# Dividing by a running sum: an exact reciprocal replaced by a guess and a cubic correction

## The reference, cut to what matters

```
x = x + 0.5 * ffn(layernorm(x));  x = x + attention(layernorm(x));  x = x + 0.5 * ffn(layernorm(x))

# ffn
h = square(relu(einsum('bsd,fd->bsf', x, W_fc)));  y = einsum('bsf,df->bsd', h, W_proj)
# 5 steps of a threshold recurrence on y, spikes counted; result = count / 5

# attention (h = layer_norm(x, gamma, beta))
keys, values = h @ Wk.T + bk, h @ Wv.T + bv
key_att = keys @ Wka.T + bka
keys_weight = exp(key_att / sqrt(128))
keys_weight = keys_weight / cumsum(keys_weight, axis=1)
pooled_keys = cumsum(keys_weight * keys, axis=1)
return pooled_keys * values
```

## Time and profile before

| what | value |
|---|---|
| median of 3 runs | 166.24 us (166.01 to 166.38) |
| the profiled execution | 166.34 us, its span 164.6 us (1.7 us lie around it) |
| granted TensorE clock, mean | 0.985 of full speed |
| busy: PE, DVE, ACT, POOL | 155.0 (94%), 136.8 (83%), 124.9 (76%), 109.5 (67%) us |

### The profile page before, as it was taken

One profiled execution on the slowest core, in us unless ns is written; L12 is line 12 of the kernel. 1 busy time (PEld: TensorE's weight loads), 2 busy tenths in 40 slices (PEclk: granted clock), 3 DMA queues, 4 the chain that ended last, 5 costly groups with the idle time before them and its releaser, 6 DMA issues.

```text
span 164.6 us, 2555 instructions
## 1 busy us (share of the span) xinstructions
PE 155.0 (94%) x767; PEld 103.2 (63%) x767; DVE 136.8 (83%) x381; ACT 124.9 (76%) x233; POOL 109.5 (67%) x165
## 2 busy tenths in 40 slices
PE   6999999999999999999999999999999999999931
PEld 6884747575767657566576665766667666565421
DVE  1785389788899999999999999999999999845541
ACT  3266789999995968758899587786784968797960
POOL 1239109899899676997999979979959475350200
PEclk9999999999999999999999999999999999999995
DMA  4890000000000000000000020000010202020222
GB/s 144 235 279 27 0 6 0 0 0 0 2 6 0 0 0 2 4 0 0 0 0 0 4 64 0 2 0 2 24 44 0 64 0 64 6 64 0 64 64 64
DMA packets 10285, 5.08 MB, mean 31 GB/s; under 512 B 1056, under 2 KB 10144, under 8 KB 10272
## 3 DMA queue, kind: packets, MB, share of 16 engines
q1 hardware_dynamic: 9744, 4.66, 9.7%
q10 hardware_dynamic: 528, 0.26, 0.5%
HBM read 2.82 MB, written 2.10 MB: 30 GB/s over the span
## 4 chain that ended last, share of the span: by engine, by line
DVE 53%; PE 38%; issue 4%; POOL 2%; ACT 1%; ACTq 0%; DVEq 0%; POOLq 0%
PE work L652 17%; DVE inv_sum L504 16%; DVE pooled L508 6%; DVE stats L427 4%; PE hidden L614 4%; DVE weight_sum L496 3%; PE hidden L618 3%; PE hidden L615 3%; DVE attended L516 3%; DVE in_lo L459 3%; PE work L626 2%; DVE stats_att L427 2%; DVE att_lo L464 2%; DVE x_second L521 2%; DVE x_att L490 2%
## 5 line engine op out<-in xcount | busy, mean ns | idle before, releaser
L652 PE MATMUL work<-square,proj_t 128*128 128x512 f32 x128 | 62.9, 598 | 0.5 <-DVE square L472 0.5
L363 ACT ACTIVATE signs<-work 128x512 bf16<-128x512 f32 x80 | 44.6, 605 | 15.6 <-PE work L652 15.6
L349 ACT ACTIVATE relu<-hidden 128x512 f32<-128x512 f32 x64 | 38.7, 605 | 7.7 <-PE hidden L618 7.6
L290 POOL TENSOR_TENSOR rstd<-var_eps,minus_half 128x4 f32<-128x4 f32 x16 | 19.9, 1242 | 21.6 <-DVE neg_mean L436 21.5
L652 PEld LDWEIGHTS work<-square,proj_t 128*128 128x128 f32 x128 | 22.1, 189 | 15.2 <-ACT square L354 5.8
L354 ACT ACTIVATE square<-relu 128x512 f32<-128x512 f32 x46 | 29.3, 636 | 0.8
L614 PE MATMUL hidden<-in_hi,fc_lo 128*128 128x512 f32 x64 | 27.8, 435 | 0.0
L504 DVE RECIPROCAL inv_sum<-weight_sum 128x256 f32<-128x256 f32 x16 | 27.6, 1736 | 0.0
L618 PE MATMUL hidden<-in_lo,fc_hi 128*128 128x512 f32 x64 | 25.4, 396 | 0.0
L615 PE MATMUL hidden<-in_hi,fc_hi 128*128 128x512 f32 x64 | 25.3, 395 | 0.0
L323 POOL TENSOR_TENSOR share_key<-share,key 128x256 f32<-128x256 f32 x16 | 15.3, 958 | 1.3
(11 more groups left out here) (83 smaller groups left out, 257.9 us busy)
## 6 DMA issues: line engine op xcount, KB each, us to landing
x_first<-_attn_hidden_states_dram SPq DMA_DIRECT2D x8, 256.0 KB, 3.9
out_dram<-x_out SPq DMA_DIRECT2D x8, 256.0 KB, 2.2
fc_raw<-in_L_ffn_W_fc_dram ACTq DMA_DIRECT2D x1, 256.0 KB, 3.9
proj_raw<-in_L_ffn_W_proj_dram SPq DMA_DIRECT2D x1, 256.0 KB, 4.0
att_raw<-in_L_attn_Wk_dram SPq DMA_DIRECT2D x1, 64.0 KB, 3.9
att_raw<-in_L_attn_Wv_dram SPq DMA_DIRECT2D x1, 64.0 KB, 3.6
att_raw<-in_L_attn_Wka_dram SPq DMA_DIRECT2D x1, 64.0 KB, 3.4
vectors<-in_L_attn_bk_dram SPq DMA_DIRECT2D x1, 0.5 KB, 3.2
```

The source lines that it names most:

```text
L290: nc.gpsimd.tensor_tensor(rstd[kind][:], var_eps[kind][:], minus_half[:], ALU.pow).then_inc(rstd_made[kind], 1)
L349: nc.scalar.activation(relu[j.lane][:, c, :], hidden[c][:], ACT.Relu).then_inc(relu_made[j.lane], 1)
L363: nc.scalar.activation(signs[j.lane][:, k, :], work[j.lane][:], ACT.Sign, bias=bias, scale=scale).then_inc(signs_made[j.lane], 1)
L652: mm = nc.tensor.matmul(work[j.lane][:], proj_t[:, c, :], square[j.lane][:, c, :], start=(c == CONTRACT_ORDER[0]), stop=(c == CONTRACT_ORD ...
```

## The change

DVE's reciprocal goes. In its place:

- ACT `att_guess`: exp of a linear function of the sum's bit pattern, read as an integer: a guess g for 1/sum within a few per cent.
- POOL `att_guess_sum`: e = sum * g, 128x512 in one instruction.
- ACT `att_off_square`: (e - centre) squared.
- DVE `att_weight_key`: (key out of PSUM + bias) * weight. ACT's `att_key` goes, and with it the tile key.
- POOL `att_guess_share`: weight_key * g, 128x512 in one instruction.
- DVE `att_near_share` and `att_share_key`: (off_square + REST) * guess_share, then (e - ROOT) times that. The two together are a cubic in e, with the sign turned; pooled subtracts instead of adding.

The new tiles guess, guess_sum, guess_share, off_square and weight_key are doubled. `att_turn` on PE now waits for DVE's weight_key of the attention before it.

```
+def inverse_form():
...
+    log_scale = -math.log(2) * 2.0**-23
+    log_bias = math.log(2) * (127 - mu) + math.log(middle)
+    return log_scale, log_bias, root, centre, c0 - centre**2
...
-            def att_shares(b, half):
-                cols = slice(half * HALF, (half + 1) * HALF)
-                pool.wait_ge(inv_made, 2 * b + half + 1)
-                if half == 0:
-                    pool.wait_ge(key_made, b + 1)
-                if b and half == 0:
-                    pool.wait_ge(pooled_made, b)
-                nc.gpsimd.tensor_tensor(share[:, cols], weight[b % ATT_SETS][:, cols], inv_sum[:, cols],
-                                        ALU.mult).then_inc(share_made, 1)
-                pool.wait_ge(share_made, 2 * b + half + 1)
-                nc.gpsimd.tensor_tensor(share_key[:, cols], share[:, cols], key[b % ATT_SETS][:, cols],
-                                        ALU.mult).then_inc(share_key_made, 1)
-
+            def att_guess_sum(b):
+                pool.wait_ge(guess_made, b + 1)
+                if b >= 2:
+                    pool.wait_ge(share_key_made, b - 1)
+                nc.gpsimd.tensor_tensor(guess_sum[b % 2][:], weight_sum[b % ATT_SETS][:], guess[b % 2][:],
+                                        ALU.mult).then_inc(guess_sum_made, 1)
+
+            def att_guess_share(b):
+                pool.wait_ge(weight_key_made, b + 1)
+                if b >= 2:
+                    pool.wait_ge(near_share_made, b - 1)
+                nc.gpsimd.tensor_tensor(guess_share[b % 2][:], weight_key[b % 2][:], guess[b % 2][:],
+                                        ALU.mult).then_inc(guess_share_made, 1)
             for i in range(FIRST_STEP, STEPS):
-                for b in attention(i - 1):
-                    att_shares(b, 0)
-                    att_shares(b, 1)
                 for j in feed_forward(i + 2):
                     ff_normalise(j)
+                for b in attention(i):
+                    att_guess_sum(b)
                 for j in feed_forward(i + 1):
                     ff_squares(j)
                 for b in attention(i + 2):
                     att_normalise(b)
+                for b in attention(i):
+                    att_guess_share(b)
...
-            def att_key(b):
-                act.wait_ge(key_mm, b + 1)
-                if b == 0:
-                    act.wait_ge(kv_bias_made, 1)
-                if b >= ATT_SETS:
-                    act.wait_ge(share_key_made, 2 * (b - ATT_SETS + 1))
-                nc.scalar.activation(key[b % ATT_SETS][:], att_work[:], ACT.Identity,
-                                     bias=kv_bias[:, 0:1]).then_inc(key_made, 1)
-
             def att_weight(b):
                 act.wait_ge(att_mm, b + 1)
                 if b == 0:
                     act.wait_ge(exp_bias_made, 1)
+                if b >= ATT_SETS:
+                    act.wait_ge(weight_key_made, b - ATT_SETS + 1)
+                    act.wait_ge(sum_made, b - ATT_SETS + 1)
                 nc.scalar.activation(weight[b % ATT_SETS][:], att_work[:], ACT.Exp, bias=exp_bias[:, 0:1],
                                      scale=KEY_SCALE).then_inc(weight_made, 1)
+
+            def att_guess(b):
+                act.wait_ge(sum_made, b + 1)
+                if b == 0:
+                    act.wait_ge(guess_consts_made, 2)
+                if b >= 2:
+                    act.wait_ge(guess_share_made, b - 1)
+                nc.scalar.activation(guess[b % 2][:], weight_sum[b % ATT_SETS][:].bitcast(I32), ACT.Exp,
+                                     bias=log_bias[:, 0:1], scale=LOG_SCALE).then_inc(guess_made, 1)
+
+            def att_off_square(b):
+                act.wait_ge(guess_sum_made, b + 1)
+                if b >= 2:
+                    act.wait_ge(near_share_made, b - 1)
+                nc.scalar.activation(off_square[b % 2][:], guess_sum[b % 2][:], ACT.Square,
+                                     bias=off_centre[:, 0:1]).then_inc(off_square_made, 1)
...
@@ -394,6 +440,8 @@
                 for j in feed_forward(i - 1):
                     ff_sign(j, 0)
                     ff_sign(j, 1)
+                for b in attention(i - 1):
+                    att_guess(b)
                 for j in feed_forward(i):
                     ff_relu(j, 0)
@@ -408,10 +456,11 @@
                 for j in feed_forward(i):
                     ff_square(j, 1)
                     ff_relu(j, 2)
+                for b in attention(i - 1):
+                    att_off_square(b)
+                for j in feed_forward(i):
                     ff_square(j, 2)
                     ff_relu(j, 3)
-                for b in attention(i):
-                    att_key(b)
                 for j in feed_forward(i):
                     ff_square(j, 3)
                 for j in feed_forward(i + 1):
@@ -496,17 +545,33 @@
...
-            def att_invert(b, half):
-                cols = slice(half * HALF, (half + 1) * HALF)
-                dve.wait_ge(sum_made, b + 1)
-                if b and half == 0:
-                    dve.wait_ge(share_made, 2 * b)
-                nc.vector.reciprocal(inv_sum[:, cols], weight_sum[b % ATT_SETS][:, cols]).then_inc(inv_made, 1)
+            def att_weight_key(b):
+                dve.wait_ge(key_mm, b + 1)
+                if b >= 2:
+                    dve.wait_ge(guess_share_made, b - 1)
+                nc.vector.scalar_tensor_tensor(weight_key[b % 2][:], att_work[:], kv_bias[:, 0:1],
+                                               weight[b % ATT_SETS][:], ALU.add,
+                                               ALU.mult).then_inc(weight_key_made, 1)
+
+            def att_near_share(b):
+                dve.wait_ge(off_square_made, b + 1)
+                dve.wait_ge(guess_share_made, b + 1)
+                if b:
+                    dve.wait_ge(share_key_made, b)
+                nc.vector.scalar_tensor_tensor(near_share[:], off_square[b % 2][:], REST, guess_share[b % 2][:],
+                                               ALU.add, ALU.mult).then_inc(near_share_made, 1)
+
+            def att_share_key(b):
+                dve.wait_ge(near_share_made, b + 1)
+                if b:
+                    dve.wait_ge(pooled_made, b)
+                nc.vector.scalar_tensor_tensor(share_key[:], guess_sum[b % 2][:], ROOT, near_share[:],
+                                               ALU.subtract, ALU.mult).then_inc(share_key_made, 1)
 
             def att_pool(b):
-                dve.wait_ge(share_key_made, 2 * (b + 1))
+                dve.wait_ge(share_key_made, b + 1)
                 nc.vector.tensor_tensor_scan(pooled[:], ones[:], share_key[:], 0.0, ALU.mult,
-                                             ALU.add).then_inc(pooled_made, 1)
+                                             ALU.subtract).then_inc(pooled_made, 1)
 
             def att_product(b):
                 dve.wait_ge(pooled_made, b + 1)
...
             for i in range(FIRST_STEP, STEPS):
                 for j in feed_forward(i - 2):
                     ff_sum_sign(j, 1)
-                for b in attention(i - 2):
-                    att_invert(b, 0)
                 for b in attention(i - 3):
                     att_add(b)
                 for j in feed_forward(i - 2):
                     ff_sum_sign(j, 2)
                 for j in feed_forward(i - 1):
                     ff_dve_square(j, 1)
-                for b in attention(i - 2):
-                    att_invert(b, 1)
                 for j in feed_forward(i - 2):
                     ff_sum_sign(j, 3)
                     ff_sum_sign(j, 4)
@@ -583,10 +646,13 @@
                         first_normalise(j)
                 for b in attention(i - 1):
                     att_sum(b)
+                    att_weight_key(b)
                 for j in feed_forward(i):
                     if j.index > 0:
                         ff_lo(j)
                 for b in attention(i - 2):
+                    att_near_share(b)
+                    att_share_key(b)
                     att_pool(b)
                     att_product(b)
                 for j in feed_forward(i - 2):
@@ -674,7 +740,7 @@
 
             def att_turn(b):
                 if b:
-                    pe.wait_ge(key_made, b)
+                    pe.wait_ge(weight_key_made, b)
                 for t in range(NT):
                     pe.wait_ge(normed_made["att"], NT * b + t + 1)
                     last = nc.tensor.transpose(att_work[:, t * P:(t + 1) * P], normed["att"][:, t, :], ident[:])
```

More of the change, by code:

```diff
@@ L17 @@
+import math
 from contextlib import ExitStack
@@ L27 @@
 BF16 = mybir.dt.bfloat16
+I32 = mybir.dt.int32
 ALU = mybir.AluOpType
@@ L130, in macaron_kernel @@
     NL = len(LEVELS)
+    LOG_SCALE, LOG_BIAS, ROOT, CENTRE, REST = inverse_form()
     RESIDUAL_STEP = 0.5 / SPIKE_STEPS
@@ L204, in macaron_kernel @@
         att_lo = [sb(f"att_lo{k}", [P, S], F32R) for k in range(ATT_SETS)]
-        key = [sb(f"key{k}", [P, S]) for k in range(ATT_SETS)]
```

(10 more changed lines are left out.)

26 lines of the change are left out of this document (23 added, 3 removed).

## The result

| | before | changed |
|---|---|---|
| median of 5 runs | 166.24 us (166.0 to 166.68) | 171.4 us (171.24 to 172.28) |
| ratio, 95% interval | | 1.0318 (1.0292 to 1.0343) |
| profiled execution, its span | 166.34, 164.6 us | 172.28, 170.2 us |

The kernel became 3.2% slower. The direction and the range of the prediction hold; its middle, 169.8, is 1.6 us short. In the profiled execution of the changed kernel the first x landed 0.7 us later than before; its other runs have spans of 169.3 to 169.6 us, so 4.9 us of span are the change's.

What follows compares the result with a forecast made beforehand. PE was taken to set the pace, with 2.9 us of stops that DVE's relief could remove. New stops of 4.3 plus 2.2 through POOL less 2.9 gave 3.6 us slower, 169.8 us; range 166.2 to 172.2.

Steps and rivals of the forecast that it cites:

- fourth rival: POOL becomes the bound, each of its reads meeting a two-input DVE instruction: 2.8 us more, 172.6; chance 0.11.
- The maximum: Six stops of PE between 40 and 140 us, 2.9 us together, the most any relief of DVE can bring.
- Step 4's turn: PE's turn of attention 4 waits for DVE's weight_key, which stands behind the running sum: a stop of 0.87 us.
- Step 4's rest: Behind that turn, the key product and a contraction wait for ACT, delayed by the guess: 0.45 us.
- Step 8's turn: PE's turn into att_work waits for weight_key: 1.04, near_share's wait for POOL 0.1, the exponential 0.2; 1.35 us in all.
- Step 6: PE's contraction waits for DVE's square, 9.14 behind the turn: a stop of 1.0 us where it was 0.63.
- The circle: POOL and DVE wait on each other, with collisions 11.6 us per full step: 0.63 over PE's work in steps 9 to 11.
- Steps 12 and 13: PE's turn back 0.3 us late in each; in step 12 another 0.3 for guess_sum ahead of POOL's square.
- The sum: Whole kernel: 4.3 us of new stops plus 2.2 through POOL less 2.9 removed, 3.6 us slower.
- Relief alone: Rival: DVE's relief counts and the waits don't; all six stops go, 163.4 us, more likely 164.8; chance 0.13.
- no circle through POOL: Rival: the new waits come, but collisions are shorter or guess_share is early; 167.7 us; chance 0.25.
- Busy time: In the changed profile, DVE's busy time down by 10 us and ACT's up by 4.

Runs made afterwards that it cites:

- weight_key_first: The changed kernel with weight_key ahead of the running sum on DVE; 169.8 us, ratio 1.0208.
- square_first: The changed kernel with POOL's feed-forward square ahead of guess_sum; 171.84 us, ratio 1.0336.
- guess_late: As square_first, and on ACT the guess stands behind the exponential and off_square behind att_hi; 179.48 us, ratio 1.0802.
- all_that_helped: The changed kernel with near_where_free and guess_late together; 181.52 us, ratio 1.0918.
- scans_from_psum: The changed kernel with both DVE scans reading their first operand from PSUM, max replacing the product with ones, so results differ; 169.92 us, ratio 1.0224.
- guess_share_early: The changed kernel with POOL's guess_share ahead of the next attention's rstd_att and normed_att; 171.91 us, ratio 1.0343.
- near_where_free: As weight_key_first, with near_share and share_key ahead of in_lo in steps 6, 12 and 13 alone; 168.0 us, ratio 1.0107.
- all_orders: The changed kernel with weight_key before the sum, square before guess_sum, guess_share before rstd_att, near_share and share_key before in_lo; 176.66 us, ratio 1.0631.
- key_part_alone: The kernel before with only weight times key moved to DVE out of PSUM, reciprocals kept; 177.33 us, ratio 1.0666.

## Why the prediction was right, and where its sizes were off

The direction came from the mechanism forecast: new waits of PE, and a collision on POOL, that cost more than the old stops gave back. The size is 1.6 us short. The measured 171.4 lies 0.1 above the forecast's own 168.7 to 171.3; the stated range holds it because it takes in half of the fourth rival.

**The maximum.** "Their sum, 2.9 us, is the most that any relief of DVE can bring" was not exceeded. Step 7, where one such stop vanished without a new one, gained 0.64 against 0.58 predicted, and DVE's 7 us bought nothing else but 0.2 in step 9 and 0.1 in step 14.

**Step 4's turn.** Predicted late by 0.87, measured 0.86; weight_key ran from 40.61, 1.14 behind the sum, for 0.72 (0.69 taken). weight_key_first took exactly this stop away.

**Step 4's rest, mis-sized.** "0.45 for the key product and a contraction that wait for ACT" was 0.72. The working thought of ACT alone. On POOL, the guess (43.91 on ACT) releases guess_sum, and the square that PE contracts at 47.06 stands behind it: guess 0.73 and guess_sum 1.28 in a row. The two ways run side by side and the longer one counts. With the square moved ahead (square_first) 0.5 of the rest remains, at ACT's exponential, about the 0.45 forecast; with the guess moved behind the exponential as well (guess_late) 0.1 remains, and nothing of the step in all_that_helped. So ACT's way was sized rightly and POOL's, 0.2 longer, was overlooked in steps 4 and 8.

**Step 8's turn, mis-sized.** Predicted 1.04 and 0.1 for near_share, measured 1.73 in all. DVE's rows between the turn and weight_key:

```profile
71.98 0.69 DVE L508 TENSOR_TENSOR in_lo<-work,in_hi 128x512 fp32r<-128x512 f32 x1 [0.82 <-ACT in_hi L381]
73.17 0.69 DVE L561 SCALAR_TENSOR_TENSOR near_share<-off_square,guess_share 128x512 f32<-128x512 f32 x1 [0.50 <-POOL guess_share L359]
73.89 0.69 DVE L568 SCALAR_TENSOR_TENSOR share_key<-guess_sum,near_share 128x512 f32<-128x512 f32 x1
74.62 1.36 DVE L573 TENSOR_TENSOR_SCAN pooled<-ones,share_key 128x512 f32<-128x512 f32 x1
...
84.17 0.73 DVE L552 SCALAR_TENSOR_TENSOR weight_key<-att_work,kv_bias,weight 128x512 f32<-128x512 f32 x1
```

"near_share will wait some 0.1 for POOL" was 0.50, and the pooled scan, beside POOL's normed, took 1.36 instead of 1.21: together 0.55 of the missing 0.59. The rest behind the turn was 0.71 where 0.2 was forecast, as in step 4. Turn and rest make step 8 2.44 instead of 1.35, the largest error of the sum.

**Step 6.** Predicted 1.0 instead of 0.63, +0.37; measured +0.61. PE has two stops here:

```profile
66.60 0.65 PE L770 MATMUL att_value<-ident,attended 128*128 128x128 f32 x4 [0.31 <-DVE attended L581]
...
69.19 1.12 PE L718 MATMUL work<-square,proj_t 128*128 128x512 f32 x2 [0.54 <-DVE square L521]
```

The first is new, but costs nothing by itself, since PE would have stood at the second until DVE's square was there in any case. The contraction was to start 9.14 behind the job's turn and started 9.34 behind it (59.85 to 69.19). Nearly all of the difference is near_share: it started at 62.91, while POOL's normed (61.51 to 63.24) was still running, and took 0.87 instead of 0.69.

**The circle.** Its parts were right: normed_att 2.71 (2.8 said), product 1.28 (1.29), near_share 0.69 there (0.69), full steps 11.53 and 11.50 (11.6). scans_from_psum shows that without the collisions of the scans they last 10.99 and 10.93. That their time runs round this circle is read from the waits in the trace (0.49 and 0.18); guess_share_early opens it but meets another stop of 0.87, and so does not test it. In step 9 it did not bind yet (11.14), so the 1.9 us over PE's 10.97 were 1.3; against the stops that it replaced that is 0.2 won in steps 9 to 11, where 0.4 lost was forecast.

**Steps 12 and 13.** In step 12 0.6 was forecast and 0.82 measured, in part by luck. The turn back, forecast 0.3 late, could have started at 132.73 and started at 133.19, 0.46 late: near_share took 0.85 here too, beside POOL's normed. The other 0.3 was for guess_sum "ahead of the square that PE contracts". There is no such square: job 12 has its first square on DVE, and POOL has none in this step. What came in its place is of the same size by chance. POOL's guess_share started first and held that DVE square:

```profile
133.39 1.29 POOL L359 TENSOR_TENSOR guess_share<-weight_key,guess 128x512 f32<-128x512 f32 x1
```

```profile
133.65 1.58 DVE L521 TENSOR_TENSOR square<-relu 128x512 f32<-128x512 f32 x1
```

That is 0.9 more for a square that takes 0.68 in step 13, with POOL idle. PE's contraction behind it came 0.2 late (135.28 instead of 135.08), and the step is 0.3 longer from there on. The collision works both ways, and the prediction counted only POOL's side. In near_where_free, where only DVE's order differs here, the square came earlier, took 1.02 and held nothing up, and the step lasts 8.97. In step 13 the turn back was 0.54 late (0.28 before), where no change was forecast: near_share, share_key and the pooled scan, beside normed, took 0.78, 0.82 and 1.36.

**The sum.** By steps, 3.5 to 3.6 predicted, 4.9 measured: 1.1 too little in step 8, 0.3 in step 4, 0.2 each in steps 5, 6, 12 and 13, less 0.5 in step 9 and 0.3 in the others. Why step 5 is longer, where nothing was forecast, stays open (its turn back starts 6.90 behind the job's turn instead of 6.71). Part of the closeness is thus luck: the middle would be 0.8 further off without the errors that point the other way. The fourth rival, POOL as the bound, came true in part: normed did meet near_share and share_key (2.94), but rstd_att still waited 0.18 for DVE behind it, so it cost nothing there. Relief alone is refuted by the late turns themselves and by weight_key_first, where step 4 falls by 0.9 with its stop; "no circle through POOL" by steps 10 and 11, 11.5 with the collisions of the scans and 11.0 without.

**Busy time.** DVE's fell by 7.0 us, 10 said, and ACT's rose by 5.0, 4 said. Some 2 of DVE's missing 3 us are records that grew: the pooled scans and the squares by 0.7 in all each, near_share and share_key together 0.6 over 0.69 apiece.

## What to carry to other kernels

Price a change by the stops of the engine that sets the pace, not by the busy time that it takes off another: 7 us less on VectorE won 0.6 us in one step, and over the others the instructions in their place, shorter but standing where others wait, lost 5.5. When an expensive instruction is replaced by a chain over three engines, write down for each link what stands behind it on its engine; here each link was short, and the squares, normalisations and turns behind them paid. Check for each step on which engine that work really stands: POOL's square was overlooked in steps 4 and 8 and counted in step 12, which has none. Reorderings do not add up: one that alone won 1.6 us, one that won 0.7 (with guess_share ahead as well) and two that by themselves changed little together lost 5.

## What the runs showed of the hardware

- A scan of VectorE over two SBUF tiles holds GpSimd off for most of its 1.2 us: four normalisations of 1.74 in all took 2.71 beside one scan, 2.94 beside two products and a scan, 4.25 in all_orders. With the scan's first operand in PSUM they took 1.75. In near_where_free normed_att was at 1.73 again and guess_share, behind it, took 2.20 beside the scan: the collision moves, its cost stays.
- Started second, VectorE is the one held: 1.58 for a square of 0.69 behind GpSimd's product, 0.87 for near_share behind the last of the normalisations.
- The granted clock, 1.00 in the middle of the kernel before, was 0.62 on the mean of 5 us in which PE was busy for 3.66, so for most of them at the lower of its levels, 1.2 GHz of 2.4; 0.70 in the next 5 us, though PE was busy throughout, and 0.78 in key_part_alone's with 3.17. So PE pays for such stops twice: twenty counts behind those of all_orders took 2.34 instead of 1.28.
- exp over the bit pattern read as int32 took ACT 0.73, as did exp over floats out of PSUM.
